# An attention and mixture-of-experts layer: GpSimd's order, one wait of ScalarE and the split of block 1's first products in the prologue

## The chip, the cores and the metric

The kernel runs on one NeuronCore of a Trainium2 chip. The metric is the device time in microseconds, the median of three runs: 1424.85 us (1424.48 to 1424.86) for the kernel before.

## What is computed

```python
xn  = layernorm(x)                                  # x: 1 x 2048 x 128, float32
q, k, v = xn @ Wq, xn @ Wk, xn @ Wv                 # 16 heads of 64
attn = softmax(q @ k.T * 64 ** -0.5, axis=-1)       # per head, 2048 x 2048
a   = (attn @ v).reshape(1, 2048, 1024) @ Wo + bo
expert = argmax(softmax(xn @ router_w.T))           # 8 experts, one for each token
f   = square(relu(xn @ fc[expert])) @ proj[expert].T
out = x + a + f
```

## The kernel before

The 16 heads are taken as 8 pairs, and the 2048 queries in 4 chunks of 512: 32 blocks `n`, each a pair of heads and a chunk of queries. A block has 16 steps `kt` of 128 keys, with both heads `h` in each. Every step computes scores transposed (keys on partitions), takes their exponentials, and adds them into OB by products with V.

Precision: Q and K are split into a high part in a rounded format and a low remainder. Q1 and K1 hold high parts and Q2 and K2 add the low ones, so that a tile of scores is two products over 128 rows (L1015, L1019). K2 and Q2 also carry, in a row of their own, a one and the negated maximum of each query (`mrow`), so the second product subtracts the maximum. For block 0 that row arrives by two transfers, `place_max(0)`, and L1019 waits for their semaphore `d_nm`.

Maxima: the negated maximum of a query must be known before its block starts. For this the products are done a second time, turned (queries on partitions, L1031 and, for block 0, L1040). VectorE reduces every tile (L714), a block having 32 units. `minus_max` (L726) folds them into nm, TensorE turns nm (`turn_max`, L1111), ScalarE copies it into `mrow` (L596), and SyncE copies that into Q2 (L314). Block n's stream of units runs `LEAD` = 8 units ahead of its scores: in block n TensorE issues, for each score tile, one unit of block n+1.

PSUM has eight banks: MB (3) for maxima, SB (3) for scores, OB and XB. In the prologue `first()` the 32 units of block 0 go in 16 pairs (`max_pair`), each over two banks, taken in turn from SB and MB (`PAIR`); VectorE reduces a pair in one instruction (L720). Other work of TensorE stands between pairs by the table `BETWEEN`: V's four chunks, Q of block 1, and the router's products.

The prologue before the pairs has these streams, each in order on its engine:

- VectorE: statistics and `rows(j)`, the scaling of quarter j of x (L772, four instructions), for j = 0 to 3, and the low part of Q of block 0 (L779).
- TensorE: `turn_x(j)` (L968), then the split products of Q and K (L1060 to L1062).
- ScalarE: `turned(j)`, two copies of a turned quarter (`xhi` L618, `xT` L619); `high_k0(c)`, the high part of K's chunk c (L625) and a plain copy `ex` of it (L627).
- GpSimd: `low_x(j)` (L463), the low part of quarter j of x; `low_k0(c)` (L469), two instructions each, the low part of K's chunk c; zeroing (L508); x plus bias (L534).
- SyncE: `spread_q0`, `spread_k0(c)` (copies of parts between partitions), loads for the next pair of heads, a signal on `d_q[0]`, then `spread_q(1)`, the rows of ones, the fill of `sorted_x` in device memory (L392), and `place_max(0)`.

ScalarE's copy of the high part of Q for block m (`high_q`, L572) overwrites `qhi`, and waits by `q_ready(act, m - 1)` until block m - 1's copies out of it have landed; for m = 1 this is the signal that SyncE gives on `d_q[0]` late in its queue.

Of the kernel before, what the change touches and what calls it, by code (L numbers as in the profile page):

```python
# [32 lines left out]
QB = 512  # L33
JB = S // QB
TB = QB // P
PAIRS = H // 2
NB = PAIRS * JB
# [48 lines left out]
LEAD = 8  # L86
UNITS = 2 * TB * JB
# [16 lines left out]
def layer(nc, x, wq, wk, wv, wo, bo, router_wT, fc, projT, out):  # L104


    with ExitStack() as ctx:
# [98 lines left out]
        def unit(n, kt, h):  # L206

            g = UNITS + 2 * kt + h + LEAD
            return n + g // UNITS, g % UNITS

        def in_ring(i):


            return i if i < 2 else (i + 1) % 3
# [50 lines left out]
        def q_ready(eng, m):  # L265
            wait(eng, d_q[m % JB], (m // JB).times(QD, QD))
# [2 lines left out]

        BETWEEN = {0: ("v", 0), 2: ("v", 1), 4: ("v", 2), 6: ("v", 3), 8: ("q", 1),  # L270
                   9: ("r", 0), 11: ("r", 1), 13: ("r", 2), 15: ("r", 3)}
        TX = [SB[0], SB[1], MB[0], MB[1]]
        START_Q, START = MB[2], [OB, SB[2], MB[2], OB]
        PAIR = [a[:, 0:2 * QB] for a in (SB_all, MB_all)]
        EARLY = 3

        ORDER = [r * JB + c for c in range(JB) for r in range(2 * TB)]

# [19 lines left out]
        with nc.Block() as block:  # L298
# [137 lines left out]
            def _(pool):  # L436
# [46 lines left out]
                def first():  # L483
                    pool.memset(res[:, :], 0.0).then_inc(g_i, 1)
                    pool.memset(eps[:, :], EPS).then_inc(g_i, 1)
                    pool.memset(ident[:, :], 0.0).then_inc(g_i, 1)
                    pool.wait_ge(g_i, 3)
                    pool.affine_select(out=ident[:, :], in_=ident[:, :], compare_op=ALU.not_equal, fill=1.0,
                                       base=0, pattern=[[-1, P]], channel_multiplier=1).then_inc(g_i, 1)
                    pool.memset(ones[:, :], 1.0).then_inc(g_i, 1)  # L490
                    pool.wait_ge(g_i, 5)

                    pool.affine_select(out=before_p[:, :], in_=ones[:, :], compare_op=ALU.is_gt, fill=0.0,
                                       base=0, pattern=[[1, P]], channel_multiplier=-1)
                    pool.memset(one_e[:, :], 1.0)
                    pool.memset(gate[:, :, 1:NT], 1.0)
                    pool.memset(gate[:, :, 0:1], 0.0)
                    for a, n, step, base in ((falling, E, -1, E), (tokens_in, NT, P, 0), (tile_no, TILES, 1, 0)):
                        ins = pool.iota(a[:, :], [[step, n]], base=base, channel_multiplier=0,
                                        allow_small_or_imprecise_dtypes=True)  # L500
                    ins.then_inc(g_i, 1)
                    pool.wait_ge(g_i, 6)


                    k_zeros, q_zeros = ([t[h][other[h], :] for t in ts for h in range(2)] for ts in (K2, Q2))

                    def zero(z):
                        pool.memset(z.bitcast(F32), 0.0).then_inc(g_z, 1)  # L508

                    for z in k_zeros[:2] + q_zeros[:2]:  # L510
                        zero(z)
                    pool.wait_ge(g_z, 4)
                    low_x(0)
                    pool.wait_ge(g_lo, 1)
                    for z in q_zeros[2:4]:
                        zero(z)
                    pool.wait_ge(g_z, 6)
                    low_x(1)
                    pool.wait_ge(g_lo, 2)
                    low_k0(0)  # L520
                    pool.wait_ge(g_k0, 2)
                    low_x(2)
                    low_x(3)
                    pool.wait_ge(g_lo, 4)
                    for c in range(1, JB):
                        low_k0(c)
                    pool.wait_ge(g_k0, 2 * JB)
                    for z in q_zeros[4:] + k_zeros[2:]:
                        zero(z)
                    pool.wait_ge(g_z, 4 + 2 * JB)  # L530
                    pool.wait_ge(d_c, 32)
                    for j in range(JB):
                        pool.wait_ge(v_xn, j + 1)
                        pool.tensor_tensor(chunk(Y, j), chunk(Y, j), under(bob[:, :], TB), ALU.add).then_inc(g_y, 1)  # L534
# [18 lines left out]
            def _(act):  # L553
# [14 lines left out]

                def high_q(m):
                    wait(act, t_q, m.times(1, 1))  # L570
                    q_ready(act, m - 1)
                    act.activation(qhi[:, :], XB[:, :], ACT.Copy, scale=SCALE).then_inc(a_q, 1)  # L572

                def kv(kind, pair, c):
# [134 lines left out]
            def _(dve):  # L709
# [160 lines left out]
                def first():  # L870
                    statistics(0)
                    rows(0)
                    statistics(1)
                    low_w(Lin(0))
                    rows(1)
                    statistics(2)
                    statistics(3)
                    rows(2)
                    low_q0()
                    rows(3)  # L880
                    for p in range(UNITS // 2):
                        maxima_pair(p)
                        if p in BETWEEN:
                            kind, c = BETWEEN[p]
                            if kind == "q":
                                low_q(Lin(c))
                    minus_max(Lin(0))
                    for u in range(EARLY):
                        maxima(Lin(1), u)
                    choose()  # L890
                    for u in range(EARLY, LEAD):
                        maxima(Lin(1), u)

                def one(n):
                    start = n.i is None and n.off == 0
                    for kt in range(NT):
                        for h in range(2):
                            m, u = unit(n, kt, h)
                            if before(m, NB):
                                maxima(m, u)  # L900
                        if kt == AT_NM and before(n, NB - 1):
                            minus_max(n + 1)
# [53 lines left out]
            def _(pe):  # L956
# [64 lines left out]
                def max_unit(m, i, u=None):  # L1021

                    u = i if u is None else u
                    h, q, c = u // (TB * JB), u // JB % TB, u % JB
                    par, k = (m // JB) % 2, m % JB
                    m0, i0 = ring_before(m, i)
                    wait(pe, v_m, UNITS if m.off == 1 and i < 2 else m0.times(UNITS, i0 + 1))
                    if i == 0 and (m.i is not None or m.off):
                        q_ready(pe, m)
                        k_ready(pe, m // JB)  # L1030
                    pe.matmul(MB[in_ring(i)][:, :], Q1[k][h][:, q * P:(q + 1) * P],  # L1031
                              K1[par][h][:, c * QB:(c + 1) * QB], start=True, stop=True).then_inc(t_m, 1)
# [80 lines left out]
                def first():  # L1113
# [34 lines left out]
                    for u in range(EARLY):  # L1148
                        max_unit(Lin(1), u)
                    turn_max(Lin(0))  # L1150
                    for u in range(EARLY, LEAD):
                        max_unit(Lin(1), u)

                def one(n):
                    start = n.i is None and n.off == 0
                    for kt in range(NT):
                        for h in range(2):
                            scores(n, kt, h)
                            m, u = unit(n, kt, h)
                            if before(m, NB):  # L1160
                                max_unit(m, u)
                        if start and kt == AT_RANK:
                            ranks()
# [66 lines left out]
```

## Time and the profile before

| | |
|---|---|
| median of the runs | 1424.85 us |
| profiled execution | 1424.59 us, span 1422.9 us |
| TensorE busy | 1393.1 us, 98% |
| VectorE busy | 1168.9 us, 82% |
| GpSimd busy | 1073.4 us, 75% |
| ScalarE busy | 738.8 us, 52% |
| TensorE's granted clock | 0.99 of full speed |

Busy time is the time in which an engine executes, not that in which it makes headway at its best: TensorE's clock has two levels, 1.2 and 2.4 GHz, and the rows call them 0.5 and 1.0. The time of the execution is 1.7 us more than its span, which begins with the first instruction and ends with the last.

### The profile page before, as it was taken

Reading aid. Unit: us, or ns where it says so; the run is one execution under the profiler, and the core shown is the slowest. Engines: PE = TensorE matmul, PEld = TensorE weight load, DVE = VectorE, ACT = ScalarE, POOL = GpSimd, SP = SyncE. Lnnn points to the kernel's source line nnn. Section 1 sums busy time; section 2 is a strip of 40 time slices with the busy share of each in tenths; the row PEclk is TensorE's granted clock in tenths of the full one; section 3 lists DMA queues with packets and bytes.
Section 4 is the critical chain, followed back from the end, with each engine's and each line's share of the span. In section 5 each row is a group of like instructions: output and inputs, shape, how many; then the busy total and the mean of one; then the engine's idle time right before and its main releaser. Section 6 shows DMA issues by size and latency. Waiting matters only on the chain.

```text
span 1422.9 us, 20074 instructions
## 1 busy us (share of the span) xinstructions
PE 1393.1 (98%) x6447; PEld 862.0 (61%) x6447; DVE 1168.9 (82%) x1528; ACT 738.8 (52%) x1318; POOL 1073.4 (75%) x850
## 2 busy tenths in 40 slices
PE   5999999999999999999999999999999999999998
PEld 4655666666656666665666566566666666665654
DVE  7789978888778788877788787887778878888897
ACT  5254555545555545555555455455545555555554
POOL 6579777767777777777777777777777777789986
PEclk9799999999999999999999999999999999999999
DMA  3423111321113211222113211132101330001000
GB/s 77 114 57 91 42 42 25 89 66 41 41 43 72 65 42 41 63 55 61 41 42 85 61 34 42 42 91 67 38 25 43 85 71 23 7 20 31 12 23 15
DMA packets 65095, 72.12 MB, mean 51 GB/s; under 512 B 8992, under 2 KB 38240, under 8 KB 64992
## 3 DMA queue, kind: packets, MB, share of 16 engines
q1 hardware_dynamic: 63968, 68.75, 19.5%
q0 software_dynamic: 1024, 2.10, 0.5%
q8 instruction: 52, 0.85, 0.3%
q14 instruction: 51, 0.42, 0.1%
HBM read 17.83 MB, written 5.11 MB: 16 GB/s over the span
## 4 chain that ended last, share of the span: by engine, by line
PE 89%; DVE 7%; ACT 1%; POOL 1%; issue 1%; SPq 1%; DMA 0%; DVEq 0%; POOLq 0%; ACTq 0%
PE OB L1053 29%; PE SB L1015 17%; PE SB L1019 15%; PE MB L1031 15%; PE XB L1090 2%; PE XB L1081 2%; PE XB L1099 2%; DVE mx L714 2%; DVE acc L737 2%; PE XB L1005 1%; PE XB L998 1%; PE XB L1060 1%; PE XB L1062 1%; POOL acc L445 1%; PE XB L1061 1%
## 5 line engine op out<-in xcount | busy, mean ns | idle before, releaser
L445 POOL TENSOR_TENSOR acc<-acc,ex 128x512 f32<-128x512 f32 x657 | 865.1, 1336 | 160.1 <-ACT ex L561 131.4
L561 ACT ACTIVATE ex<-SB 128x512 f32<-128x512 f32 x1024 | 608.2, 598 | 467.3 <-PE SB L1019 410.1
L714 DVE TENSOR_REDUCE mx<-MB 128x1 f32<-128x512 f32 x992 | 662.9, 686 | 185.0 <-PE MB L1031 182.7
L1053 PE MATMUL OB<-ex,V 128*64 128x512 f32 x2048 | 466.1, 597 | 0.0
L1015 PE MATMUL SB<-Q,K 128*128 128x512 f32 x1024 | 426.9, 417 | 0.0
L1019 PE MATMUL SB<-Q,K 128*128 128x512 f32 x1024 | 401.6, 392 | 1.6 <-DMA Q<-mrow 1.6
L1031 PE MATMUL MB<-K,Q 128*128 128x512 f32 x992 | 391.1, 395 | 6.3 <-DVE mx L714 5.9
L737 DVE TENSOR_TENSOR acc<-acc,ex 128x512 f32<-128x512 f32 x239 | 301.6, 1262 | 16.4 <-ACT ex L561 3.8
L1053 PEld LDWEIGHTS OB<-ex,V 128*64 128x64 f32 x2048 | 138.4, 137 | 270.2 <-issue 238.1
L1015 PEld LDWEIGHTS SB<-Q,K 128*128 128x128 f32 x1024 | 193.7, 189 | 139.0 <-issue 103.0
L1031 PEld LDWEIGHTS MB<-K,Q 128*128 128x128 f32 x992 | 187.3, 189 | 53.3 <-DVE mx L714 11.8
L1019 PEld LDWEIGHTS SB<-Q,K 128*128 128x128 f32 x1024 | 193.4, 189 | 32.8 <-DMA Q<-mrow 2.0
L445 POOL TENSOR_TENSOR acc<-ex 128x512 f32<-128x512 f32 x63 | 79.8, 1287 | 83.7 <-ACT ex L561 83.7
L861 DVE RECIPROCAL rd<-rd 128x256 f32<-128x256 f32 x62 | 108.0, 1742 | 0.0
L451 POOL TENSOR_TENSOR osb<-osb,rd 128x512 f32<-128x512 f32 x31 | 39.8, 1283 | 80.3 <-DVE rd L861 80.3
L601 ACT ACTIVATE osb<-OB 128x512 f32<-128x512 f32 x32 | 19.1, 598 | 101.0 <-PE OB L1053 101.0
L851 DVE SCALAR_TENSOR_TENSOR qlo<-XB,qhi 128x512 fp32r<-128x512 f32 x31 | 21.4, 691 | 18.6 <-ACT qhi L572 18.6
L1081 PEld LDWEIGHTS XB<-wraw,xT 128*128 128x128 f32 x256 | 33.9, 193 | 3.5 <-ACT V L587 0.9
L1081 PE MATMUL XB<-wraw,xT 128*128 128x128 f32 x256 | 34.1, 276 | 0.4 <-ACT V L587 0.4
L1099 PEld LDWEIGHTS XB<-wo,osb 128*128 128x128 f32 x248 | 32.4, 191 | 2.7 <-issue 0.4
L1090 PE MATMUL XB<-acc,ones 128*64 128x512 f32 x124 | 33.4, 618 | 0.0
L1099 PE MATMUL XB<-wo,osb 128*128 128x128 f32 x248 | 32.7, 275 | 0.0
(142 smaller groups left out, 612.2 us busy)
## 6 DMA issues: line engine op xcount, KB each, us to landing
Q<-qhi SPq DMA_DIRECT2D x124, 128.0 KB, 2.8
K<-khi SPq DMA_DIRECT2D x112, 128.0 KB, 2.3
Q<-qlo SPq DMA_DIRECT2D x64, 128.0 KB, 2.6
K<-klo SPq DMA_DIRECT2D x56, 128.0 KB, 2.3
w<-fc SPq DMA_DIRECT2D x23, 256.0 KB, 2.8
w<-projT SPq DMA_DIRECT2D x23, 256.0 KB, 3.5
sorted_x<-res SPq DMA_DIRECT2D x1, 1472.0 KB, 6.9
tok<-sorted_x SPq DMA_DIRECT2D x23, 64.0 KB, 1.7
```

The costliest lines, as they stand in the source:

```text
L445: pool.tensor_tensor(a[:, :], src[:, :], EX[h][ex_slot(kt)][:, :], ALU.add).then_inc(done, 1)
L561: act.activation(EX[h][ex_slot(kt)][:, :], SB[in_ring(2 * kt + h)][:, :], ACT.Exp).then_inc(a_e[h], 1)
L714: dve.tensor_reduce(mx[:, m % 2, u:u + 1], MB[in_ring(i)][:, :], AX.X, ALU.max).then_inc(v_m, 1)
L737: dve.tensor_tensor(a[:, :], src[:, :], EX[0][ex_slot(kt)][:, :], ALU.add).then_inc(sums[0][n % 2], 1)
L861: dve.reciprocal(rd[:, cols], rd[:, cols]).then_inc(v_rd, 1)
L1015: pe.matmul(tile[:, :], K1[par][h][:, keys], Q1[k][h][:, :], start=True, stop=False)
L1019: pe.matmul(tile[:, :], K2[par][h][:, keys], Q2[k][h][:, :], start=False, stop=True).then_inc(t_s, 1)
L1031: pe.matmul(MB[in_ring(i)][:, :], Q1[k][h][:, q * P:(q + 1) * P], K1[par][h][:, c * QB:(c + 1) * QB], start=True, stop=True).then_inc(t_m, 1)
L1053: mm = pe.matmul(OB[own[h], :], V[(n // JB) % 2][:, k, own[h]], EX[h][ex_slot(k)][:, :], start=(k == 0), stop=(k == NT - 1))
L1081: mm = pe.matmul(XB[:, k * P:(k + 1) * P], xT[:, tok], wraw[pair % 2][:, 2, :], start=True, stop=True)
L1090: mm = pe.matmul(XB[own[h], :], ones[:, 0:DH], acc[h][n % 2][:, :], start=True, stop=True)
L1099: mm = pe.matmul(XB[:, q * P:(q + 1) * P], on[:, q * P:(q + 1) * P], wo_s[pair % 2][:, :], start=True, stop=True)
```

## The change

There are three edits. All numbers of lines in the text are those of the kernel before.

1. GpSimd's `low_k0(0)` moves behind `low_x(2)` and `low_x(3)`.
2. ScalarE's `high_q` of block 1 waits for `d_q0`, the semaphore of `spread_q0`'s two transfers, and no longer for SyncE's signal on `d_q[0]`.
3. Of block 1's first 8 units, 2 instead of 3 stand ahead of the turning of nm and of the router's choice of experts on VectorE, 3 behind it, and 3 are left to block 0, where `units` issues two at a time in the first three places and one in each of the next three; after six places the stream is where it was. The banks of the prologue swap roles (`TX`, `PAIR`), so that the last pair lies in SB; block 1's units 0 and 1 then wait by the general rule (units 29 and 30 of block 0) and no longer for all 32.

```diff
+        def units(n, kt, h):
+
+
+            g = 2 * kt + h
+            if n.off == 0 and g < 2 * (LEAD - MIDDLE):
+                return [(n + 1, MIDDLE + 2 * g), (n + 1, MIDDLE + 2 * g + 1)] if g < LEAD - MIDDLE else \
+                    [(n + 1, LEAD + g)]
+            m, u = unit(n, kt, h)
+            return [(m, u)] if before(m, NB) else []
+
         def in_ring(i):
 
 
@@ -269,10 +279,10 @@
 
         BETWEEN = {0: ("v", 0), 2: ("v", 1), 4: ("v", 2), 6: ("v", 3), 8: ("q", 1),
                    9: ("r", 0), 11: ("r", 1), 13: ("r", 2), 15: ("r", 3)}
-        TX = [SB[0], SB[1], MB[0], MB[1]]
+        TX = [MB[0], MB[1], SB[0], SB[1]]
         START_Q, START = MB[2], [OB, SB[2], MB[2], OB]
-        PAIR = [a[:, 0:2 * QB] for a in (SB_all, MB_all)]
-        EARLY = 3
+        PAIR = [a[:, 0:2 * QB] for a in (MB_all, SB_all)]
+        EARLY, MIDDLE = 2, 5
 
         ORDER = [r * JB + c for c in range(JB) for r in range(2 * TB)]
 
@@ -517,12 +527,10 @@
                     pool.wait_ge(g_z, 6)
                     low_x(1)
                     pool.wait_ge(g_lo, 2)
-                    low_k0(0)
-                    pool.wait_ge(g_k0, 2)
                     low_x(2)
                     low_x(3)
                     pool.wait_ge(g_lo, 4)
-                    for c in range(1, JB):
+                    for c in range(JB):
                         low_k0(c)
                     pool.wait_ge(g_k0, 2 * JB)
                     for z in q_zeros[4:] + k_zeros[2:]:
@@ -568,7 +576,10 @@
 
                 def high_q(m):
                     wait(act, t_q, m.times(1, 1))
-                    q_ready(act, m - 1)
+                    if m.off == 1:
+                        act.wait_ge(d_q0, 32)
+                    else:
+                        q_ready(act, m - 1)
                     act.activation(qhi[:, :], XB[:, :], ACT.Copy, scale=SCALE).then_inc(a_q, 1)
 
                 def kv(kind, pair, c):
@@ -888,15 +899,14 @@
                     for u in range(EARLY):
                         maxima(Lin(1), u)
                     choose()
-                    for u in range(EARLY, LEAD):
+                    for u in range(EARLY, MIDDLE):
                         maxima(Lin(1), u)
 
                 def one(n):
                     start = n.i is None and n.off == 0
                     for kt in range(NT):
                         for h in range(2):
-                            m, u = unit(n, kt, h)
-                            if before(m, NB):
+                            for m, u in units(n, kt, h):
                                 maxima(m, u)
                         if kt == AT_NM and before(n, NB - 1):
                             minus_max(n + 1)
@@ -1024,7 +1034,7 @@
                     h, q, c = u // (TB * JB), u // JB % TB, u % JB
                     par, k = (m // JB) % 2, m % JB
                     m0, i0 = ring_before(m, i)
-                    wait(pe, v_m, UNITS if m.off == 1 and i < 2 else m0.times(UNITS, i0 + 1))
+                    wait(pe, v_m, m0.times(UNITS, i0 + 1))
                     if i == 0 and (m.i is not None or m.off):
                         q_ready(pe, m)
                         k_ready(pe, m // JB)
@@ -1148,7 +1158,7 @@
                     for u in range(EARLY):
                         max_unit(Lin(1), u)
                     turn_max(Lin(0))
-                    for u in range(EARLY, LEAD):
+                    for u in range(EARLY, MIDDLE):
                         max_unit(Lin(1), u)
 
                 def one(n):
@@ -1156,8 +1166,7 @@
                     for kt in range(NT):
                         for h in range(2):
                             scores(n, kt, h)
-                            m, u = unit(n, kt, h)
-                            if before(m, NB):
+                            for m, u in units(n, kt, h):
                                 max_unit(m, u)
                         if start and kt == AT_RANK:
                             ranks()
```

GpSimd in the prologue, before: the second `low_x` is followed by one `low_k0`.

```order
L463 TENSOR_TENSOR xlo<-xT,xhi 128x512 [waits a_x,g_z]
L469 TENSOR_TENSOR K_00<-ex,K_00 64x512 [waits a_k,g_lo]
L469 TENSOR_TENSOR K_01<-ex,K_01 64x512
L463 TENSOR_TENSOR xlo<-xT,xhi 128x512 [waits a_x,g_k0]
L463 TENSOR_TENSOR xlo<-xT,xhi 128x512 [waits a_x]
L469 TENSOR_TENSOR K_00<-ex,K_00 64x512 [waits a_k,g_lo]
L469 TENSOR_TENSOR K_01<-ex,K_01 64x512
```

And now GpSimd in the same place:

```order
L473 TENSOR_TENSOR xlo<-xT,xhi 128x512 [waits a_x,g_z]
L473 TENSOR_TENSOR xlo<-xT,xhi 128x512 [waits a_x,g_lo]
L473 TENSOR_TENSOR xlo<-xT,xhi 128x512 [waits a_x]
L479 TENSOR_TENSOR K_00<-ex,K_00 64x512 [waits a_k,g_lo]
L479 TENSOR_TENSOR K_01<-ex,K_01 64x512
L479 TENSOR_TENSOR K_00<-ex,K_00 64x512 [waits a_k]
L479 TENSOR_TENSOR K_01<-ex,K_01 64x512
```

Both pairs of `xlo` instructions now stand together, and all of the K instructions behind them.

TensorE at the end of the prologue and the start of block 0, before (L976 are the router's products, L1031 units of block 1, L1111 turns nm, L1015 and L1019 are a tile of scores):

```order
L976 MATMUL XB<-rw,xT 128x8 x4
L1031 MATMUL MB<-K_00,Q_10 128x512 [waits d_k0,d_q1,v_m]
L1031 MATMUL MB<-K_00,Q_10 128x512 [waits v_m] x2
L1111 MATMUL OB<-ident,nm 8x128 [waits v_nm,a_k]
L1031 MATMUL MB<-K_00,Q_10 128x512 [waits v_m] x5
L1015 MATMUL SB<-Q_00,K_00 128x512 [waits d_q0]
L1019 MATMUL SB<-Q_00,K_00 128x512 [waits d_one,d_nm0]
L1031 MATMUL MB<-K_00,Q_10 128x512 [waits v_m]
L1015 MATMUL SB<-Q_01,K_01 128x512
L1019 MATMUL SB<-Q_01,K_01 128x512
L1031 MATMUL MB<-K_00,Q_10 128x512 [waits v_m]
L1015 MATMUL SB<-Q_00,K_00 128x512 [waits a_e0]
```

And now TensorE in the same place, with the lines of the changed kernel, which are 10 higher:

```order
L986 MATMUL XB<-rw,xT 128x8 x4
L1041 MATMUL MB<-K_00,Q_10 128x512 [waits d_k0,d_q1,v_m]
L1041 MATMUL MB<-K_00,Q_10 128x512 [waits v_m]
L1121 MATMUL OB<-ident,nm 8x128 [waits v_nm,a_k]
L1041 MATMUL MB<-K_00,Q_10 128x512 [waits v_m] x3
L1025 MATMUL SB<-Q_00,K_00 128x512 [waits d_q0]
L1029 MATMUL SB<-Q_00,K_00 128x512 [waits d_one,d_nm0]
L1041 MATMUL MB<-K_00,Q_10 128x512 [waits v_m] x2
L1025 MATMUL SB<-Q_01,K_01 128x512
L1029 MATMUL SB<-Q_01,K_01 128x512
L1041 MATMUL MB<-K_00,Q_10 128x512 [waits v_m] x2
L1025 MATMUL SB<-Q_00,K_00 128x512 [waits a_e0]
```

The turning of nm stands behind the second unit, three units stand between it and the scores, and each of the first three score tiles is followed by two units.

## Rows read from the trace of the kernel before

**Rows 1.** Busy time by stretch: length, then each engine, clock, transfer share

```profile
65.40:140.00 74.60, 69.97 (x301) 40.01 (x299) 66.15 (x94) 36.13 (x63) 60.37 (x50) 1.00 0.34 84
...
186.00:230.00 44.00, 44.00 (x213) 27.56 (x211) 35.34 (x45) 23.18 (x42) 32.84 (x26) 1.00 0.13 34
```

**Rows 2.** Groups by line and form, 65.4 to 140 us, one of VectorE

```profile
L737 DVE TENSOR_TENSOR acc<-acc,ex 128x512 f32<-128x512 f32 x16 | 19.4, 1215 | 0.9
```

**Rows 3.** The timeline of VectorE, 9 to 25 us: start, length, what

```profile
9.00 1.11 DVE L772 TENSOR_SCALAR V<-Y,mean_var,rstd 128x128 f32<-128x128 f32 x4
...
16.23 4.25 DVE L772 TENSOR_SCALAR V<-Y,mean_var,rstd 128x128 f32<-128x128 f32 x4
...
24.17 1.23 DVE L720 TENSOR_REDUCE mx<-SB 128x2 f32<-128x1024 f32 x1 [3.68 <-PE SB L1040]
```

**Rows 4.** The timeline of GpSimd, 9 to 34 us

```profile
9.88 1.36 POOL L463 TENSOR_TENSOR xlo<-xT,xhi 128x512 fp32r<-128x512 f32 x1 [2.18 <-ACT xT L619]
...
16.22 2.59 POOL L469 TENSOR_TENSOR K<-ex,K 64x512 fp32r<-64x512 f32 x2 [2.39 <-ACT ex L627]
...
18.89 1.26 POOL L463 TENSOR_TENSOR xlo<-xT,xhi 128x512 fp32r<-128x512 f32 x1
...
33.01 2.63 POOL L469 TENSOR_TENSOR K<-ex,K 64x512 fp32r<-64x512 f32 x2 [3.49 <-ACT ex L627]
```

**Rows 5.** The timeline of ScalarE, SyncE and TensorE, 16 to 23 us

```profile
16.45 0.60 ACT L619 ACTIVATE xT<-MB 128x512 f32<-128x512 f32 x1
...
17.24 8.06 SPq L314 DMA_DIRECT2D K<-K  x6
...
18.15 0.60 ACT L627 ACTIVATE ex<-SB 128x512 f32<-128x512 f32 x1
...
20.55 1.12 PE L968 MATMUL MB<-ident,V 128*128 128x128 f32 x4 [4.45 <-DVE V L772]
...
22.19 0.59 ACT L619 ACTIVATE xT<-MB 128x512 f32<-128x512 f32 x1
```

**Rows 6.** The timeline of all engines, 34 to 38 us

```profile
34.12 0.39 PE L1062 MATMUL XB<-xlo,whi 128*128 128x512 f32 x1
...
35.68 0.60 ACT L572 ACTIVATE qhi<-XB 128x512 fp32r<-128x512 f32 x1 [2.27 <-SPq L381]
...
36.31 0.69 DVE L851 SCALAR_TENSOR_TENSOR qlo<-XB,qhi 128x512 fp32r<-128x512 f32 x1 [0.97 <-ACT qhi L572]
...
37.06 1.06 PE L976 MATMUL XB<-rw,xT 128*128 128x8 f32 x8 [2.05 <-DVE qlo L851]
```

**Rows 7.** Busy time in stretches of 2 us; the clock is third from the end

```profile
38.00:40.00 2.00, 2.00 (x9) 1.63 (x8) 1.06 (x2) 0.00 (x0) 1.95 (x2) 0.55 0.84 193
...
46.00:48.00 2.00, 2.00 (x10) 1.88 (x8) 2.00 (x2) 0.00 (x0) 0.69 (x1) 0.50 1.05 291
...
58.00:60.00 2.00, 2.00 (x9) 1.59 (x8) 1.81 (x4) 1.45 (x3) 0.83 (x1) 0.83 0.00 0
```

**Rows 8.** The waits of the first 60 us: total, times, longest

```profile
DVE mx L720 <- PE SB L1040: 6.7, 4, 3.7
```

**Rows 9.** The timeline of all engines, 44 to 56 us

```profile
44.24 0.58 SPq L392 DMA_DIRECT2D sorted_x<-res  x1
...
48.30 0.18 DVE L726 TENSOR_REDUCE nm<-mx 128x8 f32<-128x32 f32 x1
...
50.49 0.41 PE L1111 MATMUL OB<-ident,nm 128*8 128x128 f32 x1
...
51.24 1.34 SPq L314 DMA_DIRECT2D Q<-mrow  x2
...
55.27 0.63 PE L1019 MATMUL SB<-Q,K 128*128 128x512 f32 x1
```

**Rows 10.** The transfers of 14 to 60 us: count, size, us to landing

```profile
sorted_x<-res SPq DMA_DIRECT2D x1, 1472.0 KB, 6.9
...
K<-K SPq DMA_DIRECT2D x8, 128.0 KB, 2.3
```

## The prediction

> **What bounds the kernel now.** I first read the busy time of two long stretches [rows 1]. From 186 us on, TensorE is busy for 44.00 of 44.00 us: there it sets the pace, and what lies ahead only shifts it. Between 65.4 and 140 us TensorE is idle for 4.6 us in all while VectorE is the engine it waits for. What is won before 65 us is kept only if VectorE, and TensorE with it, start that stretch earlier; nothing in it is tied to a fixed moment. So I follow the two engines through the first 60 us. The profiled execution took 1424.59 us for a span of 1422.9; the median is 1424.85. A time won in the span is taken from 1424.85, and the 0.26 us between the two is noise. A change of under 0.2% (2.85 us) can't be told from none.
>
> **Part 1: the low parts of K behind all of x's.** VectorE scales the fourth quarter of x (`rows(3)`) in four instructions from 16.23 us. They take 4.25 us; four like them took 1.11 us at 9.00 [rows 3]. In those 4.25 us GpSimd runs `low_k0(0)`, 2.59 us from 16.22, and one `low_x`, 1.26 us from 18.89 [rows 4]: three instructions of about 1.3 us, each holding up one of VectorE's. The edit takes the first two away. GpSimd's next is `low_x(2)`, which needs ScalarE's copy that ends at 16.45 + 0.60 = 17.05 [rows 5], so it begins near 17.2, some 0.96 us after VectorE. At 9.88 GpSimd began 0.88 us after such a group, during its fourth instruction, and VectorE still took 1.11 us [rows 3, 4]. So `rows(3)` should end at 17.35 instead of 20.48.
>
> What is late next: TensorE turns this quarter over, in 1.12 us before, at 1.2 GHz [rows 5]; at 2.4 GHz an estimated 0.7, to 18.1. ScalarE is free at 18.15 + 0.60 = 18.75, and its two copies of 0.6 us, overlapping a little, end at 19.75; before, they ended at 22.8 [rows 5]. The first pair of turned maxima also needs the first K parts copied between partitions: the second of these transfers is issued at 17.24 + 0.60 and lands 2.3 us later, at 20.15 [rows 5, 10]. So the first pair starts at 20.2 and not at 22.8, 2.6 us earlier. Before, at 1.2 GHz, VectorE began 1.4 us after it, at 24.17 [rows 3]; with two products at 2.4 GHz I take 0.5 us off. VectorE begins near 21.0: 3.2 us won (2.6 if the clock is low).
>
> The moved `low_k0(0)` costs GpSimd 2.6 us, but GpSimd had waited 3.49 us ahead of the last of them, for ScalarE's copy of K [rows 4]. That cover shrinks to 0.9 us; without it, the excess would be added to the zeroing behind it.
>
> **Part 2: ScalarE's Q copy.** The high part of Q of block 1 is copied at 35.68, after 2.27 us of idle time, released by the SyncE queue, which issues K's copies and four loads first. Its product had ended at 34.12 + 0.39 = 34.51 [rows 6]. With the direct wait on `d_q0` (Q's two transfers, landed by 19) the copy runs from 34.6 to 35.2 on the old clock, before VectorE is free, which was at 36.31 - 0.97 = 35.34 [rows 6]. So the whole 0.97 us of idle time goes. The shift is now 4.2 us.
>
> **The clock.** TensorE had idled for 2.05 us until 37.06 because of this copy [rows 6], and its clock fell to 1.2 GHz just past 38 us (mean 0.55), stood at 0.50 from 46 to 48, and rose only past 58 [rows 7]. Here VectorE waited four times on products in SB, 6.7 us in all, 3.7 of it at 24.17 [rows 8]; the three others, 3.0 us together, lie at 39 to 46. After the change the idle time of TensorE is 1.0 us. Does the clock hold? Full-width products are sparse in this part, and between 46 and 48 they did not lift the clock although TensorE read as busy for 2.00 us. I take a fall after one more pair, so that the waits are 0.65, 0.8 and 1.0 us: 0.55 us won. `minus_max(0)` then comes at 48.30 - 4.75 = 43.55. If the clock holds, all three waits go, and it comes at about 41.9.
>
> The Trainium skill, "TensorE: Matmul & The Clock Gate", Part 1, has the clock as a gate which sustained matmul activity opens and idleness closes. By it the halved idle time could keep the gate open; the row at 46 to 48 speaks against reading "busy" as activity. Both cases are carried on below without the page.
>
> **Part 3: block 1's first products split.** Pair 15 now lies in SB, so block 1's first unit need not wait for its reduction: about 0.15 us. With two units instead of three ahead of it, `turn_max(0)` starts about 0.75 us after nm and not 50.49 - 48.30 = 2.19; `mrow`'s copies into Q2 then follow after 0.75 us, as before (51.24) [rows 9], at 45.1. Three units are left out ahead of block 0's first scores.
>
> Those scores' second product (L1019) waits for `mrow`. Here a new wait appears. SyncE's fill of `sorted_x` (1472 KB) is issued at 44.24 and lands 6.9 us later, at 51.14 [rows 9, 10], with the transfer engines full (1.05) from 46 to 48 [rows 7]; `mrow` went out at 51.24, just behind its end. The fill is released by GpSimd's zeroing, which follows the last K copy and so gains only part 1's 3.3 us: issued at 40.9, landed at 47.8. `mrow`, sent at 45.1 or earlier, stands in the same queue behind it and lands near 48.0; alone it would be 45.1 + 2.3 = 47.4. I take L1019 at 48.2, against 55.27 [rows 9]: 7.1 us earlier. This gate also swallows what a held clock would bring, since `mrow` lands no sooner for it. VectorE, with units 0 to 4 and the router's choice to do meanwhile, is done at about 49, when unit 5 is ready.
>
> Three units more stand behind L1019 than before. Each has 512 columns, 0.43 us at 1.2 GHz and 0.21 at 2.4; I take 0.9 us for the three. The clock rose 3.4 us after L1019 before [rows 7, 9]; I assume the like. **Sum: 7.1 - 0.9 = 6.2 us**, of which 3.2 + 0.97 + 0.55 + 0.15 = 4.9 is there at nm, and 1.3 us comes from the split. 1424.85 - 6.2 = 1418.65.
>
> **Rivals.**
> A. As worked out, 4.9 to 7.3 us won (the ends: clock and transfer each 0.6 us better or worse, the smaller one being the gain at nm alone): 1417.5 to 1420.0, best 1418.7. Chance 0.68.
>
> B. The fourth scaling instruction loses the race with `low_x(2)` and waits for all of its 1.3 us: `rows(3)` ends at 18.5, ScalarE's copies at 20.4, the first pair starts at 20.5, and the copies behind them are 0.6 us late. Through the transfer that is about 0.5 us less: 1419.2. For it: the fourth starts at about 0.8 and GpSimd at 0.96, a narrow gap. Against: the group at 9.00 [rows 3]. Chance 0.12. The Trainium skill, "SBUF — State Buffer", "Who interferes with whom", says that whichever of the two engines starts first holds the shared ports for its whole instruction. The rows at 16.2 agree; by it a `low_x` that begins ahead of the fourth costs all of its length.
>
> C. The clock is low for longer. It stays at 1.2 GHz over the first pairs and V's products (about the 1.2 us by which the last two pairs' doubled time outruns their reductions), and in block 0 it rises some 3.4 us later, which costs TensorE half of that. 6.2 - 1.2 - 1.7 = 3.3: 1421.5. Chance 0.10.
>
> D. No change that can be measured. Between 65.4 and 140 us VectorE's 16 additions average 1215 ns [rows 2], drawn out by GpSimd's. With the phases shifted, four microseconds may be lost there: about 1422.6. For it: VectorE is the bound there. Against: neither engine's order changes. Chance 0.07.
>
> E. Slower, the same place in the extreme. An addition that waits for a whole GpSimd instruction takes about 0.7 + 1.3 = 2.0 us, 0.8 more than now. This decides from the eighth of the 16; at 12 of them it is 9.6 - 6.2 = 3.4 us slower, 1428.2. Chance 0.03.
>
> That the edit does not free VectorE at all needs another cause for the 4.25 us than GpSimd; its inputs were there, and four instructions that each take as long as one of GpSimd's leave little room. It is inside C's chance.
>
> **How the numbers follow.** The likeliest is A's 1418.7. A and B hold 0.80, and with the nearer half of C and the far ends left out the range is 1417.0 to 1421.2. Faster by over 0.2% are A, B and C: 0.90; within it D: 0.07; slower E: 0.03.
>
> **What the new profile would show.** The four scaling instructions near 16.2 in about 1.1 us (2.3 in B); the first reduction of a pair near 21.0; no wait of the Q copy for the queue; nm near 43.6 (41.9 if the clock held); the first L1019 near 48.2, waiting for the transfer from `mrow`; the clock at full again near 52; the end of VectorE's stretch near 134 instead of 140. It would be wrong if L1019 comes much later than 49, or if VectorE's busy time between 59 and 134 grows.

## The result and the profile after

The changed kernel takes 1419.74 us (median of 8 runs, 1417.05 to 1421.94) against 1425.17 us for the kernel before in the same comparison (8 runs, 1424.48 to 1427.10). The ratio is 0.996, 95% interval 0.9949 to 0.9971: 5.4 us faster, by over 0.2%. The forecast was 1418.7 in a range of 1417.0 to 1421.2. The profiled execution took 1418.86 us, with a span of 1417.1 us, 5.8 us less than before.

VectorE in the changed kernel, from its timeline (start and length in us, engine, line, operation, repeat count, idle time before and what ended it). The numbers of lines are those of the changed kernel: for VectorE and for the ScalarE copies named here (`xT`, `ex`) they are 11 higher than before, for GpSimd, TensorE and SyncE 10 higher.

```profile
16.24 1.12 DVE L783 TENSOR_SCALAR V<-Y,mean_var,rstd 128x128 f32<-128x128 f32 x4
21.18 1.23 DVE L731 TENSOR_REDUCE mx<-MB 128x2 f32<-128x1024 f32 x1 [3.82 <-PE MB L1050]
...
31.96 0.68 DVE L862 SCALAR_TENSOR_TENSOR qlo<-XB,qhi 128x512 fp32r<-128x512 f32 x1
...
34.42 1.23 DVE L731 TENSOR_REDUCE mx<-MB 128x2 f32<-128x1024 f32 x1 [0.65 <-PE MB L1050]
...
36.94 1.23 DVE L731 TENSOR_REDUCE mx<-MB 128x2 f32<-128x1024 f32 x1 [0.15 <-PE MB L1050]
...
40.72 1.23 DVE L731 TENSOR_REDUCE mx<-MB 128x2 f32<-128x1024 f32 x1 [1.33 <-PE MB L1050]
...
43.12 0.19 DVE L737 TENSOR_REDUCE nm<-mx 128x8 f32<-128x32 f32 x1
...
49.37 1.29 DVE L725 TENSOR_REDUCE mx<-MB 128x1 f32<-128x512 f32 x2 [1.06 <-PE MB L1041]
```

The scaling of x's last quarter takes 1.12 us where it took 4.25 [rows 3]. The first reduction of a pair begins at 21.18 (24.17). The low part of Q, which had waited 0.97 us [rows 6], has no idle time ahead. The three waits for TensorE are 2.13 us together, where they were 3.0 [rows 8]. Two more waits of VectorE in the kernel before, on products in MB at 25.83 and 28.36 us, are gone as well. They stand in its list of waits (total, times, longest):

```profile
DVE mx L720 <- PE MB L1040: 0.6, 2, 0.4
```

nm comes at 43.12 (48.30, rows 9).

GpSimd, from its timeline of the same execution:

```profile
17.21 1.27 POOL L473 TENSOR_TENSOR xlo<-xT,xhi 128x512 fp32r<-128x512 f32 x1 [3.37 <-ACT xT L630]
19.82 1.28 POOL L473 TENSOR_TENSOR xlo<-xT,xhi 128x512 fp32r<-128x512 f32 x1 [1.33 <-ACT xT L630]
21.17 8.04 POOL L479 TENSOR_TENSOR K<-ex,K 64x512 fp32r<-64x512 f32 x6
29.70 2.63 POOL L479 TENSOR_TENSOR K<-ex,K 64x512 fp32r<-64x512 f32 x2 [0.49 <-ACT ex L638]
```

`low_x(2)` began 0.97 us after the scaling, during its fourth instruction, and did not hold it up. The moved K instructions cost nothing: GpSimd still waited 0.49 us for ScalarE ahead of the last ones (3.49 before, rows 4).

TensorE and SyncE around block 0's first scores, from the timeline of all engines:

```profile
20.37 0.69 PE L1050 MATMUL MB<-K,Q 128*128 128x512 f32 x2 [0.87 <-DMA K<-K]
...
40.95 0.58 SPq L402 DMA_DIRECT2D sorted_x<-res  x1
...
43.83 0.41 PE L1121 MATMUL OB<-ident,nm 128*8 128x128 f32 x1
...
44.57 1.99 SPq L324 DMA_DIRECT2D Q<-mrow  x2
...
48.11 0.80 PE L1029 MATMUL SB<-Q,K 128*128 128x512 f32 x1 [1.48 <-DMA Q<-mrow]
```

The first pair waited for the transfer of K, at 20.37. At 48.11 TensorE had waited 1.48 us for `mrow`, whose copies were issued at 44.57 behind the fill; issuing the two took 1.99 us instead of 1.34. The fill landed 6.8 us after its issue, near 47.7, and L1029 began 0.4 us later. Before, L1019 came at 55.27 and had no such wait [rows 9].

Busy time in stretches of 2 us (TensorE first, clock third from the end):

```profile
36.00:38.00 2.00, 2.00 (x6) 1.07 (x5) 1.84 (x2) 0.00 (x0) 1.95 (x2) 0.50 0.73 166
48.00:50.00 2.00, 1.89 (x5) 1.52 (x6) 0.94 (x3) 0.60 (x1) 0.00 (x0) 0.50 0.00 0
52.00:54.00 2.00, 2.00 (x8) 1.55 (x8) 1.91 (x5) 0.92 (x2) 0.97 (x1) 0.74 0.00 0
```

TensorE's clock fell to 1.2 GHz at 36 us and rose near 53 (before: just past 38, and past 58, rows 7). In the kernel before it had also been low from 17.7 to 24.6 us, from TensorE's wait for x's last quarter on; in the changed kernel it stayed full there. One stretch of the two, before and after:

```profile
20.00:22.00 2.00, 1.46 (x6) 1.36 (x7) 0.49 (x2) 0.30 (x1) 0.15 (x1) 0.50 0.46 103
```

```profile
20.00:22.00 2.00, 1.63 (x11) 1.57 (x12) 0.82 (x1) 1.95 (x5) 1.92 (x2) 1.00 0.48 111
```

From here on every landmark is moved by the same amount. TensorE's waits in the kernel before, and in the changed one:

```profile
96.94 0.50 PE L1019 MATMUL SB<-Q,K 128*128 128x512 f32 x1 [1.59 <-DMA Q<-mrow]
...
116.37 0.50 PE L1031 MATMUL MB<-K,Q 128*128 128x512 f32 x1 [0.90 <-DVE mx L714]
```

```profile
91.30 0.50 PE L1029 MATMUL SB<-Q,K 128*128 128x512 f32 x1 [1.61 <-DMA Q<-mrow]
...
110.77 0.50 PE L1041 MATMUL MB<-K,Q 128*128 128x512 f32 x1 [0.89 <-DVE mx L725]
```

They are 5.64 and 5.60 us earlier, like unit 16 of block 1 ahead of them (65.47 to 59.80, 5.67). VectorE's 16 additions of the matching stretch average 1218 ns (1215 before, rows 2), by this row of the groups by line and form:

```profile
L748 DVE TENSOR_TENSOR acc<-acc,ex 128x512 f32<-128x512 f32 x16 | 19.5, 1218 | 0.9
```

### The profile page after: what moved, and what is told of

It is laid out like the page before. It is cut to its first block, busy times and chain, and to the rows that moved or that the text cites. A ratio compares the mean times of both kernels' runs of the same rounds, so it can differ in the third digit from the quotient of the medians.

```text
span 1417.1 us, 20073 instructions
## 1 busy us (share of the span) xinstructions
PE 1390.8 (98%) x6447; PEld 859.8 (61%) x6447; DVE 1167.0 (82%) x1528; ACT 739.4 (52%) x1318; POOL 1073.9 (76%) x850
## 4 chain that ended last, share of the span: by engine, by line
PE 88%; DVE 6%; POOL 1%; ACT 1%; issue 1%; SPq 1%; DMA 1%; DVEq 0%; POOLq 0%
PE OB L1063 29%; PE SB L1025 16%; PE SB L1029 15%; PE MB L1041 14%; PE XB L1100 2%; PE XB L1091 2%; PE XB L1109 2%; DVE acc L748 2%; DVE mx L725 2%; PE XB L1015 1%; PE XB L1008 1%; POOL acc L455 1%; PE XB L1070 1%; PE XB L1072 1%; PE XB L1071 1%
## 5 line engine op out<-in xcount | busy, mean ns | idle before, releaser
L1029 PE MATMUL SB<-Q,K 128*128 128x512 f32 x1024 | 401.8, 392 | 3.1 <-DMA Q<-mrow 3.1
L1029 PEld LDWEIGHTS SB<-Q,K 128*128 128x128 f32 x1024 | 193.4, 189 | 35.0 <-DMA Q<-mrow 4.2
```

The costliest lines, as they stand in the source:

```text
L1029: pe.matmul(tile[:, :], K2[par][h][:, keys], Q2[k][h][:, :], start=False, stop=True).then_inc(t_s, 1)
```

## The experiments

Eleven runs were made, ten of new kernels and one of the changed kernel again, each compared with the kernel before on the same chip. The medians of that kernel were 1424.86 (first four), 1424.33 (next four) and 1424.95 (last three), so a difference of under about 0.6 us between two groups says nothing.

**The parts alone.** The first three kernels are the kernel before with one part each: `low_k0(0)` moved; `high_q` with its new wait; the split of units with the swap of banks.

> The kernel before with part 1 alone (low_k0(0) behind all low_x). My theory: GpSimd's two K instructions held up the scaling of x's last quarter; the four scaling instructions at 16.2 take 1.1 us instead of 4.25, the first reduction of a pair begins near 21.2 instead of 24.17, nm near 45.2, and the whole gains 3.0 us (2.4 to 3.6). Rival: the fourth scaling instruction or another GpSimd instruction takes its place, the group takes 2.3 us or more, and under 2.5 us is won. Second rival: the gain at nm is eaten by the transfer of mrow behind the fill of sorted_x; then L1019 has a wait on the transfer and the whole gains under 2 us.

Measured: 1421.35, ratio 0.9976 (0.9967 to 0.9985), 3.5 us faster. Timeline of VectorE:

```profile
16.22 1.11 DVE L770 TENSOR_SCALAR V<-Y,mean_var,rstd 128x128 f32<-128x128 f32 x4
21.21 1.23 DVE L718 TENSOR_REDUCE mx<-SB 128x2 f32<-128x1024 f32 x1 [3.87 <-PE SB L1038]
...
33.04 0.69 DVE L849 SCALAR_TENSOR_TENSOR qlo<-XB,qhi 128x512 fp32r<-128x512 f32 x1 [0.96 <-ACT qhi L570]
...
45.02 0.18 DVE L724 TENSOR_REDUCE nm<-mx 128x8 f32<-128x32 f32 x1
```

The scaling is freed by this edit alone, the Q wait (0.96) is left, nm is 3.28 us earlier, and the gain arrives at the end. The expectation held, and both rivals fell: L1019, here at 51.98, has no wait for the transfer.

> The kernel before with part 2 alone (ScalarE's Q copy waits for d_q0). My theory: the copy at 35.68 starts near 34.6, VectorE's 0.97 us of idle time ahead of the low part of Q goes, the low part starts near 35.35, and the whole gains 1.0 us, up to 1.5 if TensorE's clock falls later. Rival: SyncE's queue still holds up what follows (the copies of Q of block 1), so that under 0.4 us is left at nm (48.30 before).

Measured: 1423.47, ratio 0.9989 (0.9980 to 0.9998), 1.4 us faster, of which 0.96 us stands at nm (47.34); the interval reaches from 0.3 to 2.8 us. The idle time ahead of Q's low part is gone. Nothing in SyncE's queue gave it back.

> The kernel before with part 3 alone (split of block 1's first products and the swap of banks). nm is not earlier here, so the transfer of mrow (about 49.8) goes out when the fill of sorted_x has nearly landed. If the fill is what cost the split its gain in the changed kernel, L1019 comes near 52.3 instead of 55.27, with under 0.5 us of wait on the transfer, and the whole gains 1.2 to 1.8 us. Rival: VectorE's work bounds this place, not the transfer; then L1019 comes as early but the reductions at 65 us are no more than 0.6 us earlier, which is also what the changed kernel showed between nm (5.2 us earlier) and its reductions at 59.8 (5.7 us earlier).

Measured: 1422.37, ratio 0.9983 (0.9974 to 0.9992), 2.5 us faster, more than the 1.2 to 1.8 expected. Timelines of VectorE and TensorE:

```profile
48.39 0.19 DVE L736 TENSOR_REDUCE nm<-mx 128x8 f32<-128x32 f32 x1
...
62.71 1.39 DVE L724 TENSOR_REDUCE mx<-MB 128x1 f32<-128x512 f32 x2 [0.31 <-PE MB L1040]
```

```profile
52.32 0.80 PE L1028 MATMUL SB<-Q,K 128*128 128x512 f32 x1 [0.41 <-DMA Q<-mrow]
```

From nm to the reduction that follows the waits (unit 16 of block 1) are 14.32 us here and 17.17 us before (48.30 to 65.47), but 16.68 in the changed kernel (43.12 to 59.80). So the split is worth 2.9 us in this profile, where `mrow`'s copies go out behind a fill that has nearly landed, and 0.5 us in the changed kernel's. Not all of that difference is the fill: the clock rose 1.6 us after the first score product here (near 53.9), and 4.9 us after it in the changed kernel. The three parts alone sum to 3.5 + 1.4 + 2.5 = 7.4 us, and together give 5.4: some 2 us are lost where they meet. The intervals of the four medians are 1.3 to 1.6 us to each side, so the medians alone don't prove this loss. The profiles show it too: at unit 16 the parts alone are 3.30, 1.06 and 2.76 us earlier, 7.1 in all, and the changed kernel 5.7.

**Where the 2 us go.** Two kernels move the fill of `sorted_x` in the changed kernel: behind `mrow`, or to SyncE's start. In these cuts of the code the arguments of the fill are shortened.

```diff
-                    sp.dma_start(sorted_x..., under(res[:, :], TILES)).then_inc(d_res, 16)
                     place_max(Lin(0))
+                    sp.dma_start(sorted_x..., under(res[:, :], TILES)).then_inc(d_res, 16)
```

> The changed kernel with SyncE's fill of sorted_x issued behind mrow's two copies instead of ahead of them. My theory: mrow's copies stood in the queue behind the fill; now L1029 comes near 47.0 instead of 48.11 and TensorE's 1.48 us of wait shrinks to 0.4, the reductions at 59.8 come 0.8 us earlier, and the whole gains 0.5 to 1.2 us over the changed kernel (near 1418.8 against 1419.7). Rival: the two copies of mrow take as long to issue and land without the fill (the first landing at 2.3 us plus its place behind the other), L1029 stays within 0.4 us of 48.1, and nothing is won.

Measured: 1417.56 (1416.00 to 1418.27), ratio 0.9949 (0.9935 to 0.9962): 7.3 us faster than before. VectorE, SyncE and TensorE:

```profile
43.12 0.18 DVE L737 TENSOR_REDUCE nm<-mx 128x8 f32<-128x32 f32 x1
...
44.07 1.32 SPq L324 DMA_DIRECT2D Q<-mrow  x2
...
46.48 0.80 PE L1029 MATMUL SB<-Q,K 128*128 128x512 f32 x1 [0.47 <-DMA Q<-mrow]
```

L1029 comes 1.63 us earlier, and its wait shrinks from 1.48 to 0.47 us. More is won than expected. But not all of the 1.63 us is the fill. That nm is at 43.12 as in the changed kernel is chance: the clock was low from 17.5 to 24.3 us here and full from there to 44.8, while in the changed kernel it was full up to 36 us and low from there on. With the full clock the turning of nm took less, and `mrow`'s copies were issued at 44.07 instead of 44.57: 0.5 us. From that issue to L1029 are 2.41 us instead of 3.54: 1.13 us, and this is the fill's share.

```diff
+                    sp.wait_ge(g_i, 1)
+                    sp.dma_start(sorted_x..., under(res[:, :], TILES)).then_inc(d_res, 16)
                     spread_q0()
...
-                    sp.dma_start(sorted_x..., under(res[:, :], TILES)).then_inc(d_res, 16)
                     place_max(Lin(0))
```

> The changed kernel with the fill of sorted_x issued at the start, ahead of SyncE's first copies of Q and K, and so out of mrow's way. If mrow's place behind the fill is the gate, this does what issuing the fill behind mrow did: L1029 near 46.5, with 0.5 us of wait or less, and 1.5 to 2.2 us less than the changed kernel. Rival: what helped there was only where TensorE's clock happened to rise (4.9 us after the first L1029 in the changed kernel's profile, 1.7 us after it with the fill behind mrow); then the median is within 0.7 us of the changed kernel's, though L1029 comes earlier.

Measured: 1416.57 (1414.36 to 1418.35), ratio 0.9950 (0.9936 to 0.9963). In its profile TensorE's clock fell in no stretch:

```profile
36.00:38.00 2.00, 1.66 (x11) 1.14 (x10) 2.00 (x3) 0.00 (x0) 1.95 (x2) 1.00 0.91 208
48.00:50.00 2.00, 2.00 (x9) 1.52 (x9) 2.00 (x5) 1.03 (x3) 1.52 (x2) 1.00 0.00 0
```

There nm came at 41.39, the first score product with `mrow` at 44.74 after a wait of 0.96 us (46.5 and at most 0.5 had been expected, with a low clock), and the time was 1414.36. Four other executions of the same kernel, at a mean clock of 0.993 to 0.994 instead of 0.999, took 1416.47 to 1418.35. So with the same program the time went with the granted clock; where the clock stepped in those four was not recorded.

The last of the second group is the changed kernel again:

> The changed kernel once more, unaltered, for a second profile and for times on the same chip as the others. If its spread (1417.1 to 1421.9 in eight runs, where the kernel before has 1424.5 to 1427.1) comes from where TensorE's clock falls and rises, this profile has the clock's steps at other moments than 35.98 and 53.04 us, while every wait ahead of 17 us is the same, and the time differs accordingly. Rival: the spread comes from the transfers or from GpSimd and VectorE holding each other up; then the steps are where they were or the first L1029 moves by more than 0.5 us without them.

Measured: 1418.96 (1418.85 to 1420.64), ratio 0.9964 (0.9951 to 0.9978). The clock fell at nearly the same place as in its first profile (36 us, and rose near 53), so this profile says nothing on the spread. It does give a fair comparison on one chip: the fill at the start is 2.4 us better than leaving it (1418.96 to 1416.57), and no execution of the one reached those of the other. The rival, that the median would be within 0.7 us, fell. The fill behind `mrow`, 7.3 us below its kernel before where the changed kernel was 5.4 below, is about 2 us better.

**The clock.** Ten products of 512 columns that nobody uses are added ahead of the router's products, to hold the clock:

```diff
+                    def keep_busy(times):
+                        pe.wait_ge(a_k, JB)
+                        for _ in range(times):
+                            pe.matmul(OB[:, :], whi[0][:, 0, :], xhi[:, 0:QB], start=True, stop=True)
...
+                                keep_busy(4 if c == 0 else 2)
                                 logits(c)
```

> The changed kernel with ten products added whose results nobody uses (four ahead of the first router products, two ahead of each other three, all into OB), so that TensorE's clock may hold between 31 and 48 us. My prediction said that the transfer gate swallows what a held clock brings: nm comes near 41.7 instead of 43.12, but L1029 stays near 48, and the whole gains under 0.8 us over the changed kernel, unless the clock is then still full behind L1029, which would spare 0.43 - 0.23 us on each product until it rose before, some 2 us. Rival: the products do not hold the clock; then they take TensorE 0.9 us for each two, and nm comes 1 to 2 us later than 43.12.

Measured: 1418.56 (1418.17 to 1420.63), ratio 0.9961 (0.9947 to 0.9974), 0.4 us from the changed kernel on the same chip. Timelines of VectorE, SyncE and TensorE:

```profile
41.90 0.19 DVE L737 TENSOR_REDUCE nm<-mx 128x8 f32<-128x32 f32 x1
```

```profile
42.86 3.36 SPq L324 DMA_DIRECT2D Q<-mrow  x2
...
48.17 0.80 PE L1029 MATMUL SB<-Q,K 128*128 128x512 f32 x1 [3.29 <-DMA Q<-mrow]
```

This is the gate, plainly: nm is 1.22 us earlier (43.12 to 41.90), `mrow`'s copies go out 1.7 us earlier, L1029 is at 48.17 instead of 48.11, and the whole difference became wait, 3.29 us instead of 1.48.

> The same ten added products, and the fill of sorted_x behind mrow's copies. With neither gate nor low clock nm comes near 41.7, L1029 near 45.0, both 1.4 us earlier than with the fill moved alone, and the whole is 1 to 3 us faster than that one (1417.56). Rival: the clock falls in the same place all the same, and the whole is 0 to 1.5 us slower than that one.

Measured: 1416.39 (1414.74 to 1417.70), ratio 0.9943 (0.9930 to 0.9957). L1029 comes at 45.31 with 0.71 us of wait. The kernel with the same added products is 2.2 us faster with the fill behind than with it in the way (1418.56 to 1416.39). The clock held until 43.9 us and then fell all the same, and rose near 50.8. What the ten products give here is not shown: 7.9 us below the kernel before, against 7.3 us for the fill behind `mrow` without them, is within the noise of two groups.

**Both together, and the other collision.** Three kernels start from the one with the fill at the start.

```diff
+                    pool.wait_ge(v_xn, 3)
                     low_x(1)
```

> The changed kernel with the fill at the start, and GpSimd's low_x(1) held back until VectorE has scaled x's third quarter (it waits for v_xn at 3). The third quarter's four scaling instructions took 1.84 us in the changed kernel beside low_x(1), against 1.11 alone. If one GpSimd instruction with two inputs in SBUF holds up one scaling instruction, they now take 1.1 us, Q's low part comes 0.7 us earlier, and the first reduction of a pair near 20.6 instead of 21.15; the whole gains 0.5 us over the kernel with the fill at the start (0.3 to 0.7, at the edge of what can be told). Rival: low_x(1), now 0.5 us or more later, holds up K's second chunk, ScalarE's copies and the first pair, and the first reduction is not earlier than 21.15.

Measured: 1417.09, ratio 0.9946 (0.9933 to 0.9960): not faster than 1416.57. The mechanism is there all the same, in VectorE's timeline:

```profile
12.84 1.12 DVE L785 TENSOR_SCALAR V<-Y,mean_var,rstd 128x128 f32<-128x128 f32 x4
...
20.74 1.23 DVE L733 TENSOR_REDUCE mx<-MB 128x2 f32<-128x1024 f32 x1 [3.78 <-PE MB L1052]
```

The third quarter is scaled in 1.12 us instead of 1.84, and the first pair is reduced 0.4 us earlier; a gain of this size is not told from none, with the clock falling near 34 in this profile. By its low clock the profile serves for another reading. VectorE, SyncE and TensorE:

```profile
43.42 0.18 DVE L739 TENSOR_REDUCE nm<-mx 128x8 f32<-128x32 f32 x1
...
44.88 1.32 SPq L324 DMA_DIRECT2D Q<-mrow  x2
...
47.27 0.79 PE L1031 MATMUL SB<-Q,K 128*128 128x512 f32 x1 [0.34 <-DMA Q<-mrow]
...
58.51 1.37 DVE L727 TENSOR_REDUCE mx<-MB 128x1 f32<-128x512 f32 x2 [0.30 <-PE MB L1043]
```

The clock is at 0.50 from nm to behind the first scores, as in the changed kernel, and only the fill is out of the way. From the issue of `mrow`'s copies to the product that needs them are 2.39 us (3.54 in the changed kernel), and from nm to unit 16 are 15.09 us (16.68). So with a like clock at the scores the fill costs 1.15 us at that product. At unit 16 it is 1.6 us, of which a part may be the clock, which rose 3.9 us after that product here and 4.9 us after it in the changed kernel. With the fill out of the way the split is worth 17.17 - 15.09 = 2.1 us.

The other two have, on top of the ten products, three more ahead of block 0's first scores; the last one also has the late `low_x(1)`.

```diff
                     for u in range(EARLY, MIDDLE):
                         max_unit(Lin(1), u)
+                    pe.wait_ge(a_nm, 1)
+                    keep_busy(3)
```

> As the one with all, without holding back low_x(1): the changed kernel with the fill at the start and thirteen unused products. Expected 0.5 us more than the one with all, and 1.5 to 2.5 us less than the one with the fill at the start alone (1416.57) if the clock holds; the same within 0.7 us if it falls near 43 us.

Measured: 1415.38 (1414.95 to 1416.57), ratio 0.9937 (0.9923 to 0.9950). That is 1.2 us less than the kernel with the fill at the start, short of the 1.5 to 2.5 expected, or 1.8 us if each is taken against its own kernel before. In its profile the clock fell near 42.9 us, as the rival had it, and was full again from 46.4.

> The changed kernel with the fill at the start, low_x(1) held back, and thirteen products added that nobody uses: ten between the last pairs as before and three ahead of block 0's first scores, once mrow is copied. If the clock now holds through to block 0 in most executions, nm comes near 41.0, the first L1029 near 44.3, the clock is full behind it, and the median is 1413 to 1415 with a narrow spread (under 2 us). Rival: the clock falls near 43 us all the same, since VectorE's choice of experts leaves TensorE idle there; then the three products cost what they take, and the median is 1415.5 to 1417.

Measured: 1414.60 (1414.50 to 1416.59), ratio 0.9932 (0.9918 to 0.9945): the fastest median, 10.4 us faster than before, and about 5 us faster than the changed kernel, with a spread of 2.1 us. Its lead of 0.8 us over the one without the late `low_x(1)` is not told from none. In its profile (of an execution of 1415.85 us) the clock fell once, from 20 to 23 us, and was full ahead of block 0's scores and behind. With the early fall nm came at 43.10 and the first score product with `mrow` at 46.46, some 2 us later than expected; the median was where it had been expected. Its stretches:

```profile
44.00:46.00 2.00, 1.90 (x7) 1.17 (x7) 1.86 (x7) 1.32 (x2) 0.59 (x1) 1.00 0.00 1
48.00:50.00 2.00, 1.99 (x8) 1.06 (x7) 2.00 (x4) 1.50 (x3) 0.00 (x0) 1.00 0.00 0
```

So unused products pay here, once the fill is out of the way. The fair comparison is between the two kernels with the late `low_x(1)` on one chip: 1417.09 without the thirteen products and 1414.60 with them, 2.5 us, and the granted clock was 0.992 to 0.994 in the five executions without and 0.997 to 0.999 in the five with them. The share of the last three is not shown.

## Why the prediction was right

- **Part 1**: right. The scaling took 1.12 us (1.11 said), the first pair started at 20.37 (20.2), waiting for the transfer that was named, and VectorE began at 21.18 (21.0). 3.0 us came out of it instead of 3.2. Rival B's collision did not come in any of the ten profiles with this edit, all of which have 1.11 or 1.12 us; the gap of 0.97 us held.
- **Part 2**: right, 0.97 us at VectorE.
- **The clock**: it fell at 36, one pair later than I had it; the waits were 0.65, 0.15 and 1.33 us, 2.1 instead of 2.45. nm came at 43.12 (43.55 said). The rest of that difference is a term which the prediction left out: it placed all of VectorE's waits behind the first pair at 39 to 46 us, from the row for SB, and two more on MB, 0.6 us in all, were gone where the clock no longer fell from 17.7 to 24.6 us.
- **Part 3, the gate**: `turn_max(0)` 0.71 us after nm (0.75 said), L1029 at 48.11 (48.2), 7.16 us earlier than before, behind the fill. That it swallows what a held clock brings was shown by the added products: 1.2 us at nm, 0.0 at L1029. It also swallowed the prediction's own error at nm, so that 48.2 was hit although nm was 0.4 us early.
- **Mis-sized**: "I take 0.9 us for the three", with the clock's rise 3.4 us after L1029. It rose 4.9 us after it. Of the 7.16 us only 5.67 were left at the reduction of unit 16 (65.47 to 59.80), so 1.5 us went there; the rest of the chain kept 5.6. That is the difference between 6.2 and 5.6 us. Here the low clock went on for longer, in the way of the second half of rival C; its first half did not come, the clock being full from 20 to 35 us. VectorE was also done with unit 4 at 48.3 and waited 1.06 us, where I had it hardly waiting; in the two profiles with only the fill moved this wait was gone.
- **What the split was worth**: 1.3 us said; 2.5 us alone (2.9 in the profile), 0.5 in the changed kernel's profile. That the sum was nearer than this term is partly luck: nm was 5.2 us earlier instead of 4.9, and this error and that of the split have opposite signs. The median, 5.4 us faster, also stands for executions that lie 4.9 us apart, and only one of those eight was profiled.
- **Rivals D and E** did not come: the additions behind 60 us averaged 1218 against 1215 ns, and VectorE was busy for 66.2 us of the 74.6 from 59.80 on, as before from 65.40 on.

What stays open: the clock's steps are at other moments in other executions, and there is one profile for each kernel but the changed one, so the time at which the clock will fall or rise is not explained by any run here. What the fill costs is better known. By the two timed pairs (1418.96 to 1416.57, and 1418.56 to 1416.39) it is 2.2 to 2.4 us in all. By the profiles 1.1 us of this is the wait of L1029, and 1.6 us is lost by unit 16. The rest would be what the clock's later rise costs, and this is not shown. Nor does any run tell whether `mrow`'s copies waited for their turn in SyncE's queue or for the transfer engines, which the fill kept full (270 to 290 GB/s from 42 to 46 us): all runs issue both from SyncE.

## What to carry to other kernels

When several streams of a prologue are brought forward together, look for the one that is brought forward less. Here a large transfer that nobody awaited yet was issued ahead of 4 KB that the first scores awaited. It came 3.3 us earlier and the 4 KB 6.7 us earlier, so what had been hidden became a wait. Put such a fill where its queue is idle. And run the parts alone: where their sum is more than the whole, compare the profiles for a wait that only the whole has. Compare profiles at a like clock, or the clock's step is taken for the effect.

## What the runs showed of the hardware

- Four VectorE scaling instructions took 4.25 us beside three two-input GpSimd instructions of 1.3 us, 1.84 us where one such instruction was under way at their start, and 1.12 us where it began 0.97 us after them, during the last of the four.
- The moments at which TensorE's clock steps between its two levels differ from profile to profile of nearly the same program: it fell near 17.5 and 45, near 20, near 34, at 36, or in no stretch, and the same kernel took 1414.4 us at a mean clock of 0.999 and 1416.5 to 1418.4 at 0.993 to 0.994. The changed kernel's runs spread over 4.9 us, those of the split alone over 1.4.
- In the changed kernel TensorE read as busy for 2.00 of 2.00 us in the stretches from 36 to 44 us, where pairs of 512 columns alternate with router products of 8, and the clock stayed at 0.50. With ten added products of 512 columns among them it was 1.00 there and fell at 42.9 to 43.9 us, in three profiles. In two profiles without them, those with only the fill moved, it stayed at 1.00 there too.
- The issuing of `mrow`'s two copies took 1.99 us where it began 3.6 us after the fill was issued, and 3.36 us where it began 1.9 us after; at 4.7 us after, with the fill still under way, it took 1.34 us, as without it.
- From the issue of these copies (2 KB each) to the product that waits for them were 2.39 to 2.47 us where the fill had gone, had nearly landed or came later, 3.54 us with it issued 3.6 us ahead, and 5.31 us with it issued 1.9 us ahead.
